# An audio tower on one core: the convolution with the band as moving operand, attention's centring folded into its weights, w1 loaded once and copied on chip, another set of PSUM banks for the first group's convolution, and a new order of steps

## The reference

```
tok:   out = tanh(tanh(x W_in0 + b) W_in1 + b);  out = |core| * out * out
       out = tanh(tanh(out W_out1 + b) W_out0 + b)
       h   = convolution over tokens, 15 taps, zero padding 7, stride 2  -> (8, 375, 64)
attn:  n = (h - mean) / sqrt(var + eps)            over the features
       q, k, v = n Wq^T, n Wk^T, n Wv^T
       logits = q k^T, zero above the diagonal;  a = relu(logits) / max(row, 1)
       h = h + (a v) Wo^T
ffn:   n = layernorm(h);  two best of 16 experts by n gate_w + gate_b, softmax over the two
       expert e: relu(n w1[e] + b1[e]) w2[e] + b2[e]      (64 -> 128 -> 64)
       h = h + layernorm(n + sum of gate * expert) * gamma + beta
```

## Time and profile before

| | us |
|---|---|
| median of 3 runs | 189.54 |
| lowest, highest | 185.79, 190.82 |
| the profiled execution's own time | 186.72 |
| its span, first to last instruction | 184.8 |
| TensorE busy | 159.4 |
| VectorE busy | 104.9 |
| ScalarE busy | 92.9 |
| mean granted TensorE clock | 0.979 |

### The profile page before, as it was taken

One profiled execution on the slowest core, in us unless ns is written; L12 is line 12 of the kernel. 1 busy time (PEld: TensorE's weight loads), 2 busy tenths in 40 slices (PEclk: granted clock), 3 DMA queues, 4 the chain that ended last, 5 costly groups with the idle time before them and its releaser, 6 DMA issues.

```text
span 184.8 us, 4222 instructions
## 1 busy us (share of the span) xinstructions
PE 159.4 (86%) x1594; PEld 91.9 (50%) x1594; DVE 104.9 (57%) x422; ACT 92.9 (50%) x149; POOL 29.7 (16%) x46
## 2 busy tenths in 40 slices
PE   5999999597695999999979999999999949979710
PEld 5887677255683465434544535455444424446310
DVE  0322632296769879853676885439896246172132
ACT  0356669164434645555466556654556534636410
POOL 8960020021303212000032000001400002000030
PEclk9999999969999999999999999999999999999995
DMA  3556478400000791004985005795000699320001
GB/s 96 116 88 166 126 191 178 83 0 2 4 0 15 218 253 38 4 10 94 243 220 122 5 10 138 209 238 141 0 5 10 173 227 248 75 45 0 0 0 42
DMA packets 16111, 17.72 MB, mean 96 GB/s; under 512 B 8421, under 2 KB 12353, under 8 KB 15964
## 3 DMA queue, kind: packets, MB, share of 16 engines
q1 hardware_dynamic: 14928, 16.74, 35.9%
q10 hardware_dynamic: 844, 0.64, 1.1%
q0 software_dynamic: 320, 0.09, 1.1%
HBM read 16.49 MB, written 0.97 MB: 94 GB/s over the span
## 4 chain that ended last, share of the span: by engine, by line
PE 42%; issue 15%; SPq 13%; DVE 12%; DMA 10%; POOL 4%; ACT 1%; POOLq 1%; DVEq 0%
PE z L1052 13%; PE y L1066 12%; DMA w_last<-last_row 6%; SPq L398 5%; PE a L992 4%; DMA gate_all<-gates_dram 3%; POOL stat_A L581 3%; PE a L982 2%; DVE h L758 2%; SPq L326 2%; SPq L367 2%; PE a L1013 1%; PE z L1028 1%; DVE halves_A L630 1%; PE a L998 1%
## 5 line engine op out<-in xcount | busy, mean ns | idle before, releaser
L528 ACT ACTIVATE hid<-z 128x750 f32<-128x750 f32 x64 | 50.8, 797 | 36.3 <-PE z L1052 29.1
L1052 PE MATMUL z<-xg,w_s 64*64 64x375 f32 x512 | 55.0, 479 | 1.6 <-DVE xg L850 1.6
L1066 PE MATMUL y<-hid,w_s 64*64 64x375 f32 x512 | 53.5, 480 | 0.7 <-ACT xg L438 0.4
L850 DVE TENSOR_TENSOR xg<-xa_t,gate_all 128x375 f32<-128x375 f32 x60 | 31.9, 546 | 20.9 <-PE z L1052 11.8
L1052 PEld LDWEIGHTS z<-xg,w_s 64*64 64x64 f32 x512 | 20.3, 132 | 20.5 <-issue 14.5
L1066 PEld LDWEIGHTS y<-hid,w_s 64*64 64x64 f32 x512 | 19.4, 132 | 19.7 <-issue 11.3
L581 POOL TENSOR_TENSOR stat_A<-stat_A,minus_half 125x6 f32<-125x6 f32 x4 | 6.2, 1561 | 57.1 <-DVE stat_A L763 57.1
L581 POOL TENSOR_TENSOR stat_F<-stat_F,minus_half 125x6 f32<-125x6 f32 x4 | 5.8, 1440 | 51.5 <-DVE stat_F L640 51.5
L587 POOL TENSOR_TENSOR stat_t<-stat_t,minus_half 125x6 f32<-125x6 f32 x4 | 6.4, 1598 | 40.9 <-DVE stat_t L729 40.9
L863 PE MATMUL a<-ident 128*128 128x128 f32 x56 | 10.2, 344 | 1.6 <-POOL ident L543 1.6
L863 PEld LDWEIGHTS a<-ident 128*128 128x128 f32 x56 | 8.9, 245 | 2.7 <-POOL ident L543 1.6
(11 more groups left out here) (163 smaller groups left out, 205.0 us busy)
## 6 DMA issues: line engine op xcount, KB each, us to landing
gate_all<-gates_dram SPq DMA_DIRECT2D x54, 187.5 KB, 4.1
gate_all<-gates_dram SPq DMA_DIRECT2D x12, 93.8 KB, 2.8
w_s<-in_L_ffn_w_dram SPq DMA_DIRECT2D x2, 504.0 KB
w_last<-last_row SPq DMA_DIRECT2D x2, 504.0 KB
x_in<-in_x_dram SPq DMA_DIRECT2D x4, 187.5 KB
out_dram<-y_out SPq DMA_DIRECT2D x7, 93.8 KB
...
```

What stands on the lines that cost most here:

```text
L528: act.activation(hid[:, n % HID], z_pair[e % 2][:, :, 0:TO], ACT.Relu).then_inc(hid_ready.sem, 1)
L850: nc.vector.tensor_tensor(xg[:, n % XG], xa_t[g % 2][:], gate_all[:, e], ALU.mult).then_inc(xg_ready.sem, 1)
L1052: ins = mm(z[e % 2][b][q, 0:TO], w1_s[f, e, q], xg[f, n % XG], start=True, stop=True)
L1066: ins = mm(y[h][b * D:(b + 1) * D, 0:TO], w2_s[q, e, :], hid[q, (E * g + e) % HID, b], start=e == 0, stop=e == E - 1)
```

## The change

- Convolution: the tile of tokens (125 x 128) is now the stationary operand, a piece of the band the moving one. Its output has the features on the partitions, ut. Six products a group, of 122, 125, 70, 128, 70 and 66 columns. ScalarE copies ut (T5), TensorE transposes it (three products, T6) and ScalarE copies hres. Group zero uses a0 and a1 for this, so y is free once its biases are added.
- Attention: centring is a product with a fixed matrix, so it goes into the weights. VectorE sums each row of Wq, Wk, Wv and subtracts the mean (S4). Query, keys and values come from the uncentred ut and hres; the tiles xc and xn_t, their transposes and copies are gone. The variance is still needed.
- w1: one load and one broadcast of the last row on 63 partitions; after the subtraction SyncE copies each four experts' part to the other 64 partitions, by a DMA in SBUF. The first product of each four experts waits for it.
- x of groups one to three is loaded in another token order, 512 bytes a piece instead of 1536 (group zero as before), and group one is no longer cut in two by partitions. ScalarE's copy becomes contiguous.
- The filter's padded row and the band are shorter (265 instead of 626 columns), and their issues move. F4 is cut in F4 (scaled) and F6 (y_out). The lists have a new order, with 22 warm-up products instead of 28.

```diff
-        MID = 368
-        BANDW = MID + TAPS // 2 + 2 * TOK + 1
...
+        PAD = TAPS // 2
+        first = [max(0, (TOK * c - PAD + 1) // 2) for c in range(NT)] + [TO]
+        stop = [min(TO, (TOK * (c + 1) - 1 + PAD) // 2 + 1) for c in range(NT)]
+        for m in range(NR):
+            stop[2 * m] = first[2 * m + 2]
+        lead = [max(TOK * m - first[2 * m + k] for m in range(NR)) for k in range(2)]
...
+        def conv_banks(g):
+
+            return (a0, a1) if g == 0 else banks_of(g)
...
             "sync": """
-                A0.12 A1.12 A2.12 F0.5 A3.12 F1.5 F2.5 F3.5""",
+                S0.10 S0.11 S0.12 S0.13 A0.12 A1.12 F0.5 A2.12 F1.5 A3.12 F2.5 F3.5""",
...
+            if g:
+                src = x[PAIR * g + b].rearrange("(c p s) d -> p c s d", c=NR, s=2)
...
+            def setup(_, s):
+                sp.wait_ge(w1_ready, s - 9)
+                es = slice(PIECE * (s - 10), PIECE * (s - 9))
+                sp.dma_start(w1_s[D:P, es], w1_s[0:D, es]).then_inc(ld_copy[s - 10], 16)
...
             for b in range(PAIR):
-                load_x(sp, 1, b, (0, SPLIT, TOK))
+                load_x(sp, 1, b)
...
-            for b in range(PAIR):
-                at, last = slice(b * D, b * D + DX), slice(b * D + DX, (b + 1) * D)
-                sp.dma_start(w1_s[at], w1[:, 0:DX, :].rearrange("e h f -> h e f")).then_inc(ld_w1, 16)
...
+            sp.dma_start(w1_last[:].rearrange("h e f -> h (e f)"),
+                         last_row[:].rearrange("e f -> (e f)").partition_broadcast(DX)).then_inc(ld_w1, 16)
...
+            sp.dma_start(w1_s[0:DX], w1[:, 0:DX, :].rearrange("e h f -> h e f")).then_inc(ld_w1, 16)
...
                 elif s == 5:
                     act.wait_ge(conv_done.sem, conv_done.after(g, 1))
-                    if g == 0:
-                        act.wait_ge(ln_cent["T"].sem, ln_cent["T"].after(g, 1))
+                    act.copy(ut[g][:], conv_banks(g)[0][:, 0:TO]).then_inc(ut_ready.sem, 1)
+                elif s == 6:
+                    act.wait_ge(h_turned.sem, h_turned.after(g, 1))
                     act.copy(hres[g][:].rearrange("p j d -> p (j d)"),
-                             banks[0][0:TOK, 0:NJ * D]).then_inc(hres_ready.sem, 1)
+                             conv_banks(g)[1][0:TOK, 0:NJ * D]).then_inc(hres_ready.sem, 1)
...
+                elif s == 4:
+                    dve.wait_ge(ld_attn, 48)
+                    nc.vector.tensor_reduce(w_sum[:], w_in3[:], AX.X, ALU.add).then_inc(mid_ready, 1)
+                    dve.wait_ge(mid_ready, 1)
+                    nc.vector.scalar_tensor_tensor(out=w_mid[:], in0=w_sum[:].unsqueeze(2).broadcast_to([D, 3, D]),
+                                                   scalar=-1.0 / D, in1=w_in3[:], op0=ALU.mult, op1=ALU.add).then_inc(mid_ready, 1)
...
-                    for r in range(NR):
-                        if r < 2:
-                            pe.wait_ge(tanh4.sem, tanh4.after(g, r + 1))
-                        cs = [c for c in range(2 * r - 1, 2 * r + 3) if 0 <= c < NT]
-                        for c in cs:
-                            ins = mm(banks[0][0:TOK, r * P:(r + 1) * P], conv_w[:, c - 2 * r + 1, :], by_tile(buf_b[g])[:, c, :],
-                                     start=c == cs[0], stop=c == cs[-1])
+                    for c in (0, 2, 1, 4, 3, 5):
+                        if c in (0, 4):
+                            pe.wait_ge(tanh4.sem, tanh4.after(g, 1 + c // NR))
+                        at = first[c] - TOK * (c // 2) + lead[c % 2]
+                        ins = mm(conv_banks(g)[0][:, first[c]:stop[c]], by_tile(buf_b[g])[:, c, :],
+                                 conv_w[:, c % 2, at:at + stop[c] - first[c]], start=c == 0, stop=c == NT - 1)
...
-                    pe.wait_ge(w1_ready, e // PIECE + 1)
+                    pe.wait_ge(ld_copy[e // PIECE], 16)
```

More of the change, by code:

```diff
@@ L69, in signal @@
             return Signal(sem(name), per, unit)
-        MID = 368
-        BANDW = MID + TAPS // 2 + 2 * TOK + 1
-        assert BANDW + TOK <= ROW and MID + TAPS // 2 >= 3 * TOK
+        PAD = TAPS // 2
[4 more added lines that the diff above has]
+        lead = [max(TOK * m - first[2 * m + k] for m in range(NR)) for k in range(2)]
+        SPAN = max(stop[2 * m + k] - TOK * m + lead[k] for m in range(NR) for k in range(2))
+        MID = 2 * TOK
+        tops = [MID + PAD + TOK * k + 2 * lead[k] for k in range(2)]
+        BANDW = max(tops) + 1
+        assert BANDW + TOK <= ROW and min(tops) >= 2 * SPAN
         ident = sb("ident", [P, P])
@@ L85, in audio_tower @@
         filt_pad = nc.dram_tensor("filt_pad", [1, ROW], F32)
-        band = sb("band", [TOK, 640])
-        conv_w = sb("conv_w", [TOK, 4, TOK])
-        wq_s = sb("wq_s", [D, 1, D])
-        wk_s = sb("wk_s", [D, D])
-        wv_s = sb("wv_s", [D, 1, D])
+        band = sb("band", [TOK, BANDW])
+        conv_w = sb("conv_w", [TOK, 2, SPAN])
+        w_in3 = sb("w_in3", [D, 3, D])
+        w_sum = sb("w_sum", [D, 3])
+        w_mid = sb("w_mid", [D, 3, D])
         wo_s = sb("wo_s", [D, D])
@@ L120, in audio_tower @@
         hres = [sb(f"hres{i}", [TOK, NJ, D]) for i in range(NG)]
-        xc1 = [sb(f"xc1_{i}", [TOK, NJ, D]) for i in range(NG)]
+        ut = [sb(f"ut{i}", [P, TO]) for i in range(NG)]
         xv1 = [sb(f"xv1_{i}", [TOK, NJ, D]) for i in range(NG)]
@@ L196, in audio_tower @@
         gate_blank = sem("gate_blank")
-        w1_blank = sem("w1_blank")
+        ld_copy = [sem(f"ld_copy{k}") for k in range(E // PIECE)]
+        ld_b1 = sem("ld_b1")
         ld_row = sem("ld_row")
@@ L434, in setup @@
                     act.wait_ge(vec_turned, 2)
+                elif s == 3:
+                    act.dma_start(bias_last[:, 0, :], b_out[0].partition_broadcast(TOK)).then_inc(ld_bias, 16)
+                    act.wait_ge(ld_filt, 48)
+                    shifts = bass.AP(filt_pad, 0, [[1, TOK], [1, BANDW]])
+                    act.dma_start(band[:, 0:BANDW], shifts).then_inc(ld_band, 16)
             def early(_, e):
@@ L669, in setup @@
                     dve.wait_ge(ld_band, 16)
-                    for k in range(4):
-                        nc.vector.tensor_copy(conv_w[:, k, :], conv_block(k)).then_inc(conv_w_ready, 1)
+                    for k in range(2):
+                        nc.vector.tensor_copy(conv_w[:, k, :], band[:, tops[k]:tops[k] - 2 * SPAN:-2]).then_inc(conv_w_ready, 1)
                 elif s == 6:
@@ L903, in stage_t @@
                     if g == 3:
[L904 removed]
+                        pe.wait_ge(biased4.sem, biased4.after(0, 2))
                     pe.wait_ge(x_in_ready[g], 32 * PAIR)
@@ L954, in stage_t @@
-                    ins.then_inc(conv_done.sem, 1)
-            def stage_a(g, s):
-                if s == 0:
-                    pe.wait_ge(ln_cent["T"].sem, ln_cent["T"].after(g, 1))
-                    if g:
-                        pe.wait_ge(xat_ready.sem, xat_ready.after(g - 1, 1))
-                    for r in range(NR):
-                        ins = nc.tensor.transpose(a0[:, r * TOK:(r + 1) * TOK],
-                                                  xc1[g][:, PAIR * r:PAIR * (r + 1)].rearrange("p b d -> p (b d)"),
-                                                  ident[0:TOK, 0:TOK])
-                    ins.then_inc(xn1_turned.sem, 1)
-                elif s == 1:
+                        pe.wait_ge(conv_w_ready, 2)
@@ L967, in stage_a @@
                     if g == 0:
                         pe.wait_ge(prod_ready, 2 * PAIR)
-                    pe.wait_ge(xn1t_ready.sem, xn1t_ready.after(g, 1))
-                    mm(a0[:, 0:TO], w_qk[:], xn1_t[:], start=True, stop=True).then_inc(q_done.sem, 1)
+                    pe.wait_ge(ut_ready.sem, ut_ready.after(g, 1))
+                    for r in range(NR):
+                        ins = nc.tensor.transpose(conv_banks(g)[1][0:TOK, r * P:(r + 1) * P], ut[g][:, r * TOK:(r + 1) * TOK], ident[:])
@@ L971, in stage_a @@
+                    ins.then_inc(h_turned.sem, 1)
+            def stage_a(g, s):
+                if s == 1:
+                    if g == 0:
+                        pe.wait_ge(prod_ready, 2 * PAIR)
+                    else:
+                        pe.wait_ge(xat_ready.sem, xat_ready.after(g - 1, 1))
+                    pe.wait_ge(ut_ready.sem, ut_ready.after(g, 1))
+                    mm(a0[:, 0:TO], w_qk[:], ut[g][:], start=True, stop=True).then_inc(q_done.sem, 1)
                 elif s in (2, 3):
@@ L975, in stage_a @@
                             pe.wait_ge(gates_t_ready.sem, gates_t_ready.after(g - 1, 1))
+                        else:
+                            pe.wait_ge(hres_ready.sem, hres_ready.after(0, 1))
                     else:
```

148 lines of the change are left out of this document (64 added, 84 removed).

## The result

| | before | after |
|---|---|---|
| median of four runs, us | 188.18 | 173.97 |
| lowest, highest | 185.79, 190.82 | 172.33, 186.13 |
| profiled execution, its span | 186.72, 184.8 | 174.27, 172.5 |
| mean granted TensorE clock | 0.979 | 0.966 |

The ratio is 0.931, 95% interval 0.917 to 0.945: faster, 174.0 where 174.5 was predicted and within the range. (The run of 186.13 had a mean clock of 0.842; the ratio leaves it out.)

The account below looks back on a forecast made before the run. TensorE, busy 159.4 of 184.8 us, was taken as the bound. 184.8 - 3.0 - 4.8 - 1.3 - 5.3 = 170.4 us of span, 172.3 as profiled execution; median put at 174.5, range 169.5 to 183.

Parts of the forecast that it names:

- To the end of the convolution: Start to group zero's convolution end: convolution starts at 16.4 to 17.4, takes 1.5 us, ends 3.0 us earlier.
- To the gates: From group zero's convolution to its transposed gates: 29.5 us instead of 34.3, a gain of 4.8 us.
- w1 in at 26 to 28, no wait over 0.5: In the front, w1 transfers land at 26 to 28 us instead of 35.6, with no wait over 0.5 us.
- rival (b): Front: w1 lands late through x's small pieces and few DMA engines, costing 4 to 7 us; 179 us, chance 0.11.
- TensorE's work: From group zero's convolution to its gates: TensorE's steps take 27.6 us, plus 1.9 us for hand-offs.
- (a): Front: hand-offs between engines leave holes, losing half of 4.8 + 3.0 and 1.35 us of low clock; 179.5 us, chance 0.15.
- (d): TensorE between 18.4 and 48 us: the front stays at 1.2 GHz, 200 us, slower; chance 0.03.
- First experts: From group zero's transposed gates to its fifth expert: 1.3 of 1.95 us idle time goes, a gain of 1.3 us.
- To the last product: From the fifth expert to the last product: idle 7.25 becomes about 2.5 us, transposes save 0.6; gain 5.3 us.
- The 2.65 and 1.60: TensorE's late waits for group three's gate load (2.65 us) and group one's stores (1.60 us): both were to go.
- The 0.5 for SyncE: Late part: 0.5 us left for SyncE holding group three's gate transfers behind y_out and two stores.
- three signs of being wrong: Group zero's gates transposed after 52 us, w1 landing after 30, or granted clock below 0.9 for several 5 us stretches.

Follow-up runs that it names:

- run 2: The changed kernel with x of groups one to three cut at 112 partitions; median 168.23 us, ratio 0.900 to the kernel before.
- run 4: The changed kernel with biases ahead of band and attention weights, wo transpose behind the convolution, six warm-up products ahead of it; 172.36 us, ratio 0.921 to the kernel before.
- run 12: The changed kernel, unchanged, run again; median 172.43 us, ratio 0.913 to the kernel before.
- run 3: The changed kernel with the old token order of x for groups one to three, in 1536-byte pieces, uncut; 170.89 us, ratio 0.911 to the kernel before.
- runs 1: The changed kernel with six more warm-up products on TensorE between group zero's last layer and the wo transpose; 171.85 us, ratio 0.917 to the kernel before.
- run 5: The changed kernel with SyncE's old order of stores; median 171.75 us, no ratio could be given.

## Why the prediction was right, and where it was not

**To the end of the convolution, 3.0 forecast, 1.7 measured.** The start was right (17.15, upper end of 16.4 to 17.4, with the forecast's reason, only that VectorE stands 3.02 us for band and 0.46 for the attention weights instead of about one). The size of the convolution was right at full clock: 1.35 us from one to the next in groups one to three, 1.52 alone in run 2, for the 1.5 taken from the row. (My lower bound, 1.2 "strictly by columns", is miscounted: 581 / 1280 of 2.3 is 1.04.) The estimate of 1.3 from the Trainium skill (TensorE: Matmul & The Clock Gate, LDWEIGHTS) is nearer to the 1.35 than my 1.5. What was missed is the 1.48 us hole on wo_s and the lower clock behind it, 1.07 us of the convolution (2.59 less 1.52). But none of this term reaches the gates, neither the gain nor the loss, because w1 covers it: run 4 shows it for the gain, and run 12 for the loss, where the cover is just used up.

**To the gates, 4.8 forecast, 5.4 measured, and wrong in two terms that cancel.** The step that failed is "w1 in at 26 to 28, no wait over 0.5". It came at 32.9, after a wait of 3.59 us. The bytes were scaled at the old pace (30.4 us times 2.3 / 3.5 from 5.2 is 25.2, not quite the 26 stated), and the pace fell: in 15 to 20 us it is 107 GB/s, where the kernel before moved 155 and the cut x moves 196.

```profile
15.00:20.00 5.00, 4.77 (x60) 3.27 (x50) 2.68 (x12) 3.84 (x6) 0.00 (x0) 1.00 0.50 155
```

The prediction priced this as rival (b), and gave it 28.5 to 30 by the rule of the Trainium skill that the next sentence names; it was 3 to 4 us later still. The Trainium skill (DMA: Bandwidth & Descriptors, Why a DMA increments its semaphore by 16 and not by 1) would have 5 engines for 125 rows; the trace agrees: the DMA share of 0.36 in 15 to 20 us is 5.8 of 16 engines, and 112 + 13 rows instead of 125 alone brought w1 from 32.93 to 25.57 and the share to 0.68. The small pieces count as well: with the old ones and no cut, nothing waited for w1 at 29.70 (run 3). The two do not add up to shares, since each alone also lets SyncE issue w1 earlier (16.00 and 13.37 for 20.45). Why in runs 1, 4 and 5 w1 came 2 us earlier than in the two runs of the changed kernel stays open; at most 0.5 us of it is an earlier issue (19.93 to 20.32).

The other term is TensorE's work: 27.6 us for its steps, and 1.9 for hand-offs. With w1 in time it is 25.3 in all, 25.06 of them busy (run 2). Part of the excess can be named: two layers side by side start 0.68 to 0.71 us apart where 0.8 was taken nine times, and the convolutions 1.35 apart for 1.5 three times, together 1.4 of the 2.5 us; the rest is spread over steps that I did not take apart. So 29.5 forecast stands against 25.3, plus 3.6 lost to w1 and the clock: 28.9. By the tables 2.1 of the 3.6 is longer busy time at the lower clock (27.18 for 25.06) and 1.5 idleness. In this term the number is right by luck: two errors of about 4 us cancel.

Of the rivals, (b) is the one that happened. Held against run 2, the slow loads cost 5.96 us at the gates (48.58 less 42.62) and 6.2 of span, where 4 to 7 were said for a late w1. But 2.4 of the 5.96 us are there already when the convolution ends (19.7 for 17.3), so the price fits in part by chance. It was to give 179 and gave 174, mainly for my excess in TensorE's work. (a), the hand-offs, did not come about: with w1 in time TensorE idles 0.24 us there. (d) did not either: the low clock held for two stretches of 5 us and cost nothing at the gates, as long as w1 covered it (in run 3, without that cover, 1.8 us of busy time).

**First experts, 1.3 forecast, 0.7 measured.** Idle time fell from 1.95 to 0.71, 1.24 as forecast, but the stretch holds 0.54 us more work, which the new order took from the later one.

**To the last product, 5.3 forecast, 4.5 measured.** Work fell by 1.34 (0.6 forecast for the two transposes, 0.54 moved out). Idle time fell to 4.1 instead of 2.5. The 2.65 and 1.60 went as said; 1.30 at in1.2 is new, behind A2.5 on VectorE, and not foreseen; 0.39, 0.38, 0.34 and 0.34 are small hand-offs. The 0.5 for SyncE was not needed, and the move of its stores, to which the prediction put the 1.60, is not what removes it (run 5).

**The median** was put between the profile's 172.3 and 1.5% above it. The span came out 2.1 us over its forecast (172.5 for 170.4), and the 2.2 us that 174.5 has over 172.3 were hardly needed: profile and median are 174.27 and 173.97, and the runs again gave 172.43. That 174.5 lies within 0.6 us of the result is luck in this part too.

**By its own signs** the prediction is right in the start of the convolution (17.15), the gates (48.58), the first expert (51.16 for "near 50") and the stores, which nothing waits for. It is wrong in the convolution's 1.5 us (2.59), in w1's wait (3.59 for at most 1) and in the idle time after the fifth expert (4.1 for below 3.5). Two of its three signs of being wrong came: w1 landed after 30, and the granted clock fell below 0.9 in two stretches of 5 us. The range holds; the account of the front does not.
